# The last mixture of experts: fp32 one-hot rows and undivided fp32 rows in place of three bf16 parts

## The reference, cut to what matters

```python
def moe_apply(x, combine, dispatch, W, b):
    disp = jnp.einsum('sec,sd->ecd', dispatch, x)      # rows of tokens into slots
    h = jnp.einsum('ecd,edf->ecf', disp, W) + b[:, None, :]
    return jnp.einsum('sec,ecf->sf', combine, h)       # weighted, back to tokens

# x: (2, 512, 128) -> 4 groups of 256 tokens; E = 24 experts, C = 22 slots each
def per_group(xf, lw, lb):
    combine, dispatch = top2_dispatch(xf, Wg, C)
    h = moe_apply(xf, combine, dispatch, W1, b1)       # (256, 512)
    h = layer_norm(h, lw, lb)
    h = jax.nn.relu(h)
    return moe_apply(h, combine, dispatch, W2, b2)     # (256, 128)
out = jax.vmap(per_group)(xg, ln_hid_w, ln_hid_b)
return layer_norm(out + x, ln_out_w, ln_out_b)
```

## Time and profile before

| | |
|---|---|
| Runs | 462.73, 463.72, 465.2 us, median 463.72 |
| Profiled execution | 462.69 us, its span 460.9 us |
| TensorE busy, weight loads | 354.5 us (77%), 209.4 us (45%) |
| VectorE, ScalarE, GpSimd busy | 264.5 us, 201.7 us, 114.1 us |
| Mean granted clock of TensorE | 0.885 |
| Moved by DMA | 46.01 MB, mean 100 GB/s |

### The profile page before, as it was taken

How to read it: one execution, slowest core, us unless ns; L and a number is a source line. 1 busy time by engine, 2 the same in 40 slices (tenths; PEclk the granted TensorE clock), 3 DMA queues, 4 the chain that set the end, 5 groups by cost and what they waited for, 6 DMA issues and landing times.

```text
span 460.9 us, 6703 instructions
## 1 busy us (share of the span) xinstructions
PE 354.5 (77%) x2495; PEld 209.4 (45%) x2495; DVE 264.5 (57%) x661; ACT 201.7 (44%) x317; POOL 114.1 (25%) x155
## 2 busy tenths in 40 slices
PE   1797302995189899899999799987873899989970
PEld 0576301995133322233221467554463443677850
DVE  5425500332687598788950758544568947883435
ACT  2332100321040477677778458564624335565210
POOL 2000277156050716311110000010000055462232
PEclk9997555998579999999999779999995799899987
DMA  4599114001326656000000000001999467431232
GB/s 113 152 192 320 46 52 117 13 33 40 105 63 181 143 144 160 1 3 2 2 2 2 0 0 1 1 1 36 371 329 290 148 201 248 152 106 37 60 82 46
DMA packets 35876, 46.01 MB, mean 100 GB/s; under 512 B 4778, under 2 KB 21682, under 8 KB 35844
## 3 DMA queue, kind: packets, MB, share of 16 engines
q1 hardware_dynamic: 33156, 38.57, 29.9%
q0 software_dynamic: 2688, 7.02, 5.3%
HBM read 31.67 MB, written 13.78 MB: 99 GB/s over the span
## 4 chain that ended last, share of the span: by engine, by line
PE 58%; DVE 15%; issue 8%; ACT 6%; DMA 6%; POOL 5%; SPq 1%; POOLq 0%; DVEq 0%; ACTq 0%
PE ps L1397 9%; PE ps L1605 6%; PE ps L1591 5%; PE ps L1566 4%; PE ps L1851 4%; PE ps L1515 3%; PE ps L1574 3%; PE ps L1696 3%; PE ps L1880 3%; DVE early L1210 3%; PE ps L1527 2%; POOL disp_d L538 2%; PE ps L1801 2%; DVE xn L982 2%; PE ps L1786 2%
## 5 line engine op out<-in xcount | busy, mean ns | idle before, releaser
L1210 DVE TENSOR_REDUCE early<-ps 128x1 f32<-128x512 f32 x128 | 81.0, 684 | 15.9 <-PE ps L1566 11.7
L755 ACT ACTIVATE R<-ps 128x1024 f32<-128x1024 f32 x64 | 62.7, 1020 | 24.7 <-PE ps L1591 23.7
L1397 PE MATMUL ps<-ident,R 128*77 128x128 f32 (+1 forms) x224 | 35.3, 296 | 31.8 <-DMA R<-disp_d 24.8
L1397 PEld LDWEIGHTS ps<-ident,R 128*77 128x77 f32 (+1 forms) x224 | 26.7, 152 | 50.4 <-DMA R<-disp_d 25.2
L1566 PE MATMUL ps<-R 72*128 72x512 bf16 x112 | 39.0, 382 | 1.1 <-DVE early L1210 0.2
L1591 PE MATMUL ps<-R 75*128 75x512 bf16 x128 | 37.6, 379 | 1.6 <-DMA R<-R 1.3
L621 POOL DMA_INDIRECT R<-h_d,srow x16 | 16.5, 1033 | 77.3 <-DMA h_d<-ff 70.3
L1605 PE MATMUL ps<-R,vaug 128*9 128x512 f32 x256 | 33.5, 595 | 0.6 <-ACT R L755 0.6
L1179 DVE TENSOR_SCALAR R<-ps,vcol 128x256 f32<-128x256 f32 x16 | 7.0, 479 | 37.7 <-PE ps L1515 37.7
L1566 PEld LDWEIGHTS ps<-R 72*128 72x128 bf16 x112 | 10.8, 96 | 33.1 <-DVE early L1210 23.9
L538 POOL DMA_INDIRECT disp_d<-R,srow x16 | 15.9, 993 | 36.7 <-DVE srow L1125 32.1
(11 more groups left out here) (324 smaller groups left out, 696.2 us busy)
## 6 DMA issues: line engine op xcount, KB each, us to landing
R<-in_L_ffn_W_dram SPq DMA_DIRECT2D x1, 6144.0 KB, 19.9
h_d<-R SPq DMA_DIRECT2D x12, 256.0 KB, 2.8
q_d<-R SPq DMA_DIRECT2D x24, 96.0 KB, 1.9
R<-k_d SPq DMA_DIRECT2D x24, 96.0 KB
R<-q_d SPq DMA_DIRECT2D x8, 288.0 KB
R<-in_L_ffn_w_dram SPq DMA_DIRECT2D x1, 2048.0 KB, 17.1
h_d<-ff SPq DMA_DIRECT2D x6, 256.0 KB, 2.5
disp_d<-R SPq DMA_DIRECT2D x1, 1032.0 KB, 12.8
```

What stands on the lines that cost most here:

```text
L755: s.activation(probs[idx % 4], ps[:, 2 * (idx % 2):2 * (idx % 2) + 2, :].rearrange("p b t -> p (b t)"), ACT.Exp, scale=QK_SCALE).then_inc( ...
L1210: v.tensor_reduce(mcol[:, u, col:col + 1], bank(ring_bank("row", n)), AX.X, ALU.max).then_inc(s1_max, 1)
L1397: return m.transpose(dst, src, ident[0:k, 0:k])
```

## The change

The token rows `xn` and the inner rows `hsum` go into the dispatches as they are, in fp32, and `slot1h` is fp32 as well. The divisions fall away on ScalarE, VectorE and GpSimd, with their semaphores and with the homes of the parts. `slot1h` takes twice the room: seven tiles lie in R0, the eighth in `wx`. The inner rows get eight homes, one for each q; the last two lie where the weights of the first product were, so rows 6 and 7 wait until all first products are done. Each dispatch has one fp32 matmul where there were three bf16 ones. The wait of a hidden group is on `hid_z` (normalised) in place of `hid_p3`.

```diff
-        yparts = R0[:, 4096:5632].bitcast(BF16).rearrange("p (i t d) -> p i t d", i=3, t=T)
-        slot1h = [R0[:, 5632 + CG // 2 * i:5632 + CG // 2 * (i + 1)].bitcast(BF16) for i in range(T)]
+        slot1h = [R0[:, 4096 + CG * i:4096 + CG * (i + 1)] for i in range(T - 1)]
...
-        hsum = [flat(tile)[:, F1 * i:F1 * (i + 1)] for tile in (t2, attn) for i in range(2)]
...
+        slot1h.append(wx[:, :, :].rearrange("p w d -> p (w d)")[:, 0:CG])
+        hsum = [tile[:, F1 * i:F1 * (i + 1)] for tile in (
+            flat(t2), flat(attn), vaug[:, :, :, :].rearrange("p t h d -> p (t h d)"), r1(4096 + 3 * E1 * M1, 2 * F1)) for i in range(2)]
...
@@ GpSimd
-            def last_rest(u):
-                pool.wait_ge(hid_p2, u + 1)
-                g.tensor_tensor(hparts[u % 6][:, 2, :], hsum[u % 4], hparts[u % 6][:, 1, :], ALU.subtract).then_inc(hid_p3, 1)
...
-                if q >= 2:
-                    last_rest(q - 2)
-            last_rest(T - 2)
-            last_rest(T - 1)
...
@@ ScalarE
-                act.wait_ge(ln_out, 5 * T + TB * (b + 1))
-                s.copy(half_of(yparts[:, 0], b), half_of(xn, b)).then_inc(y_parts, 1)
-            for b in range(B):
-                act.wait_ge(y_rest, b + 1)
-                s.copy(half_of(yparts[:, 1], b), half_of(t2, b)).then_inc(y_parts, 1)
...
-            hid_norm(0)
             copy_quad(12)
-            hid_middle(0)
             copy_quad(13)
             hid_std(1)
...
@@ VectorE
-            for i, left in enumerate((xn, t2)):
-                for b in range(B):
-                    dve.wait_ge(y_parts, B * i + b + 1)
-                    rest = yparts[:, 2] if i else t2
-                    v.tensor_tensor(half_of(rest, b), half_of(left, b), half_of(yparts[:, i], b), ALU.subtract).then_inc(y_rest, 1)
...
-                    if q >= 4:
-                        dve.wait_ge(hid_p3, q - 3)
...
+                if q >= 6:
+
+                    dve.wait_ge(h1_mm, BLOCKS * QUADS)
...
@@ TensorE
-                    for part in range(3):
-                        for half in range(2):
-                            ins = m.matmul(ps[:, 6 * (gr % 2) + half, 0:CG // 2], yparts[:, part, gr + TB * b, :],
-                                           slot1h[gr + TB * b][:, half * (CG // 2):(half + 1) * (CG // 2)],
-                                           start=(b == 0 and part == 0), stop=(b == B - 1 and part == 2))
+                    for half in range(2):
+                        ins = m.matmul(ps[:, 6 * (gr % 2) + half, 0:CG // 2], xn[:, gr + TB * b, :],
+                                       slot1h[gr + TB * b][:, half * (CG // 2):(half + 1) * (CG // 2)],
+                                       start=(b == 0), stop=(b == B - 1))
...
-            def dispatch_hidden(gr, f, b, part):
+            def dispatch_hidden(gr, f, b):
                 for half in range(2):
                     ins = m.matmul(ps[:, chunk_bank(4 * gr + f) + half, 0:CG // 2],
-                                   hparts[(2 * gr + b) % 6][:, part, f * P:(f + 1) * P],
+                                   hsum[2 * gr + b][:, f * P:(f + 1) * P],
...
-                pe.wait_ge(hid_p3, 2 * gr + 2)
+                pe.wait_ge(hid_z, 2 * gr + 2)
...
-            pe.wait_ge(hid_p3, T - 1)
-            for part in range(3):
-                for f in range(3):
-                    dispatch_hidden(gr, f, 0, part)
...
+            for b in range(B):
+                pe.wait_ge(hid_z, T - 1 + b)
                 for f in range(3):
-                    dispatch_hidden(gr, f, 1, part)
...
+                    ins = dispatch_hidden(gr, f, b)
+                    if b == B - 1:
+                        ins.then_inc(hdisp_mm, 1)
```

More of the change, by code:

```diff
@@ L1325, in _ @@
                 v.tensor_copy(ring[slot], bank(W1_BANKS[i % 3])).then_inc(h1_dve, 1)
-            def first_rest(u):
-                dve.wait_ge(hid_p1, u + 1)
-                v.tensor_tensor(hsum[u % 4], hsum[u % 4], hparts[u % 6][:, 0, :], ALU.subtract).then_inc(hid_r1, 1)
-            for q in range(T + 1):
-                u = q - 1
+            for q in range(T):
+                t = paired[q]
                 if q == 2:
-                    first_rest(u)
                     add_bias_rows()
-                if q < T:
-                    t = paired[q]
-                    dve.wait_ge(gathered[t], 32)
-                    dve.wait_ge(hb_mm, q + 1)
-                    if q >= 4:
-                        dve.wait_ge(hid_p3, q - 3)
-                    me.link(v.scalar_tensor_tensor(out=hsum[q % 4], in0=got1[q % 4][:, 0, :], scalar=g1[:, 0, t:t + 1],
-                                                   in1=bank(BIAS_BANK[q]), op0=ALU.mult, op1=ALU.add))
-                    second = me.step(v.scalar_tensor_tensor(out=hsum[q % 4], in0=got1[q % 4][:, 1, :], scalar=g1[:, 1, t:t + 1],
-                                                            in1=hsum[q % 4], op0=ALU.mult, op1=ALU.add))
-                if q >= 1 and q != 2:
-                    first_rest(u)
-                if q < T:
-                    me.wait(second)
-                    me.link(v.bn_stats(st6[:, q, :], hsum[q % 4]))
-                    me.link(v.bn_aggr(mv[:, q, :], st6[:, q, :]))
-                    v.tensor_scalar(tmp8b[:, q:q + 1], mv[:, q, 1:2], MOE_EPS, None, ALU.add).then_inc(hvar, 1)
-                if q < T:
-                    dve.wait_ge(hstd, q + 1)
-                    me.link(v.reciprocal(rstd[:, q:q + 1], tmp8[:, q:q + 1]))
-                    v.tensor_scalar(hsum[q % 4], hsum[q % 4], mv[:, q, 0:1], rstd[:, q:q + 1], ALU.subtract,
-                                    ALU.mult).then_inc(hid_z, 1)
@@ new lines, in _ @@
+                dve.wait_ge(gathered[t], 32)
+                dve.wait_ge(hb_mm, q + 1)
+                if q >= 6:
+                    dve.wait_ge(h1_mm, BLOCKS * QUADS)
+                me.link(v.scalar_tensor_tensor(out=hsum[q], in0=got1[q % 4][:, 0, :], scalar=g1[:, 0, t:t + 1],
+                                               in1=bank(BIAS_BANK[q]), op0=ALU.mult, op1=ALU.add))
+                me.link(v.scalar_tensor_tensor(out=hsum[q], in0=got1[q % 4][:, 1, :], scalar=g1[:, 1, t:t + 1],
+                                               in1=hsum[q], op0=ALU.mult, op1=ALU.add))
@@ L1359, in _ @@
+                me.link(v.bn_stats(st6[:, q, :], hsum[q]))
+                me.link(v.bn_aggr(mv[:, q, :], st6[:, q, :]))
+                v.tensor_scalar(tmp8b[:, q:q + 1], mv[:, q, 1:2], MOE_EPS, None, ALU.add).then_inc(hvar, 1)
+                dve.wait_ge(hstd, q + 1)
+                me.link(v.reciprocal(rstd[:, q:q + 1], tmp8[:, q:q + 1]))
+                v.tensor_scalar(hsum[q], hsum[q], mv[:, q, 0:1], rstd[:, q:q + 1], ALU.subtract, ALU.mult).then_inc(hid_z, 1)
             c = 4 * NG - 1
@@ L1919, in _ @@
             for b in range(B):
-                for part in range(3):
-                    ins = dispatch_hidden(gr, 3, b, part)
+                ins = dispatch_hidden(gr, 3, b)
             ins.then_inc(hdisp_mm, 1)
```

42 lines of the change are left out of this document (3 added, 39 removed).

## The result

The changed kernel took 472.06 us in the median of its runs (466.85 to 475.89), the kernel before 464.14 us (462.73 to 465.2) beside it; the ratio is 1.0133 with a 95% interval of 1.0069 to 1.0197. The change makes the kernel slower by some 6 us (0.0133 x 464.14; the medians differ by 7.9). The forecast was 470.6 us, its range 464.8 to 473.0. The profiled execution of the changed kernel took 475.89 us, the longest of its runs and a slow one, while those of the kernel before and of e_after are fast ones. Its first token dispatch starts at 365.31 us where it started at 357.73 before: ahead of it TensorE is busy for 278.0 us with 1459 matmul records, where the same number took 271.2 us before, at a mean granted clock of 0.86 in place of 0.88, in work whose matmuls the change leaves alone.

The account below looks back on a forecast made before the run. The prediction took TensorE to bound the kernel from the first token dispatch on. Its terms, 0.9 + 0.9 + 6.9 - 1.8 = +6.9 us on the median of 463.72, gave 470.6 us, range 464.8 to 473.0.

Parts of the forecast that it names:

- What bounds the region: From first token dispatch to last second product, TensorE is the bound; the removed division is exposed for only 1.8 us.
- A record of fp32: In the dispatches, 264 fp32 columns take 0.223 us per record, two records per matmul: 0.108 us more per replacement.
- the sum of 6.9 for the hidden dispatches: Four hidden groups of 16 fp32 matmuls, 64 at 0.108 us more each, cost 6.9 us.
- The second token pair: Token dispatches of groups 2 and 3, at the full clock: 8 x 0.108 us, a cost of 0.9 us.
- The first token pair: Token dispatches of groups 0 and 1, partly at the low clock until 362.10: cost 0.9 us, up to 1.7.
- Weight loads and one-hot rows at nothing: In the dispatches, fp32 weight loads stay hidden, cost 0; writing one-hot rows in fp32 costs -0.1 to +0.1, taken as 0.
- The waits that go, -1.8: TensorE's waits for GpSimd's division before the first two hidden groups, 0.34 and 1.48 us, vanish: gain 1.8 us, bounds 0 to 1.8.
- One low stretch stays as it is: The low clock from 392.8 to 396.2, inside the first hidden group, keeps its 1.7 us loss; a second would add 1.7.
- the third rival: Around the first hidden group, one more low clock stretch costs 1.7 us, slower records 1.9: 472.3, at most 474; chance 0.10.
- The first rival: TensorE's slow stretch before the last block's copies moves or ends with 160 fewer instructions ahead: 465.1 us; chance 0.16.
- the second rival: In the dispatches, fp32 with one-hot rows takes one pass per record: about 453 to 455 us, faster below 0.158; chance 0.06.
- the fourth rival: TensorE is not the bound and freed engines give more than 1.8 us, at most 2 more: 468.6 us; chance 0.06.

Follow-up runs that it names:

- e_after: The changed kernel run again with no edit, beside the kernel before: 469.91 us, ratio 1.0141.
- e_divide: The changed kernel with the inner rows' division put back on three engines, its parts unused, and hidden groups waiting for it: 472.94 us, ratio 1.0186.
- e_one_part: The kernel before with only the first of three bf16 parts dispatched, the division still running: 463.95 us, ratio 0.9992.
- e_before_wide: The kernel before with the bias matmuls run over 128 partitions, not 24, the added ones times zeros: 459.77 us, ratio 0.9956.
- before with the shorter hold: The kernel before with block 1's gathers held only until quad 3 of the last block is done: 464.19 us, ratio 1.0069.
- e_before_all: The kernel before with 128-partition bias matmuls, 15 dummy matmuls ahead of the first dispatch, and block 1's gathers held until all second products are done: 460.25 us, ratio 0.9963.
- e_before_hold: The kernel before with block 1's gathers held back until TensorE has done all the second products: 462.96 us, ratio 0.9996.
- e_after_dose: The changed kernel with block 0's four gathers moved later, so eight gathers run beside the dense second products: 476.15 us, ratio 1.0256.
- both shorter holds: Each kernel with block 1's gathers held two quads less than until all second products are done: changed kernel 472.41 us, kernel before 464.19 us.
- e_after_wide: The changed kernel with the bias matmuls run over 128 partitions, not 24, the added ones times zeros: 464.9 us, ratio 1.0101.

## Why the prediction was right, step by step

**What bounds the region.** Right for work added: the inner rows' division put back costs some 2 to 3 us (e_divide), while every fp32 group costs its full step. For work taken away it does not hold in the same way: e_one_part gained nothing.

**A record of fp32.** Predicted 0.223 us, measured 0.2225 from start to start at the full clock and 0.440 at the low one. Groups 1, 2 and the last one cost +1.81, +1.82 and +1.91 against 1.73 each: the sum of 6.9 for the hidden dispatches came out as some 7.3. The second token pair cost +0.93 against 0.9.

**The first token pair.** Predicted +0.9 (0.9 to 1.7), measured +0.47 in the ledger. The form did cost what was said: a bf16 pair whose clock rose 3.0 us after its start took 4.29 us (e_before_wide, 356.22 to 359.2), the fp32 pair whose clock rose after 3.3 us took 5.43. But before, the clock rose only after 4.4 us. I held that instant fixed and allowed for a later one only as a loss; an earlier one gives some back. In e_after the same 16 records took 5.97 us.

**Weight loads and one-hot rows at nothing.** Right: 32 records and their loads in 7.39 us, 7.12 of it the records' own pace, leave next to nothing of the loads bare, and the wait for the one-hot rows ahead of the first dispatch is 3.54 us, where it was 3.63.

**The waits that go, -1.8.** Right: no wait before either hidden group, -0.34 and -1.53; the transposes gave 0.27 of it back.

**One low stretch stays as it is.** Wrong, and it is the third rival that happened. In the earlier trace rows it is 3.4 us long; after it is 6.8 us, 399.3 to 406.1, and it is as long in the four further profiles whose work up to there is the changed kernel's (395.5 to 402.3, 393.1 to 399.9, 397.3 to 404.1, 398.6 to 405.4) and in e_divide (394.8 to 401.6). Priced at 1.7 us it shows as +1.0 in the last biases and +0.5 in group 0. That it hangs on the thin matmuls is shown by the four profiles of wide forms, which have none, where all ten with thin ones have it. That it lengthens because of the change is likely but not certain: before with the hold it was 3.4 us, before with the shorter hold 3.4 and later another of 6.8.

**Why the total was still right.** The extra 1.5 us of low clock and 0.4 of the hidden form were set off by what I had not booked: 0.43 less for the first tokens (the earlier clock), 0.50 in block 0's second product, and 1.06 in the tail. The 0.50 is a short pause (from 415.5 on in the kernel before) that e_before_wide and e_before_all have too and e_before_hold has not, though its edit touches nothing there: scatter, and not the change. Most of the 1.06 is another pause, 0.43 us beside block 0's gathers, behind which the small matmuls start again at 430.96, 0.91 us after the last of these gathers had ended. In the changed kernel GpSimd, free of the divisions, ends them at 436.09, 9.5 us before that stage. So this part may be a gain of the freed engines that I had not seen; e_before_wide has no such pause, so it isn't shown. The forecast of +6.9 against +6.84 is thus closer than its terms are; about 2 us of it met by luck. In e_after the same distance is +7.40.

**The tail.** The bursts stayed, as forecast, but the reason was open. GpSimd's gathers beside the 32-column matmuls bring them on. In the earlier trace rows and in the copies above the loss is 4.6 us (9.86 - 5.24) and 4.3 (9.50 - 5.24). The first rival asked whether 160 fewer instructions ahead could move it: e_after_dose shows that the place in the stream does not decide. I also read the earlier trace rows wrongly: 443.54 is not when the last block's first four quads were done. Matmuls and weight loads of the kernel before:

```profile
430.96 8.69 PE L1880 MATMUL ps<-R 128*32 128x128 f32 x294 [0.43 <-issue]
...
439.22 0.17 PEld L1880 LDWEIGHTS ps<-R 128*32 128x32 f32 x6 [0.38 <-issue]
...
443.53 1.28 PEld L1880 LDWEIGHTS ps<-R 128*32 128x32 f32 x33 [1.26 <-issue]
```

The four quads end with the 288th of the 352 matmuls, which started before 438.9. The copy came more than 4 us later, within 0.02 us of the even pace's return: the slow stretch holds ScalarE up as well. The 4.6 us lost stand, since the last copy does follow TensorE's end.

**The fast fp32 form, the second rival.** Refuted by the 0.2225 us. Its threshold had a sign wrong: with 1.8 us of waits won, the two forms are even at (0.3375 + 1.8/80)/2 = 0.180 us a record, not at 0.158, where some 3.6 us would already be won. The measured record is above both.

**The freed engines, the fourth rival.** Their 9.8, 9.0 and 10.1 us (predicted 12, 9 and 9) bought the waits above and at most the pause in the tail.

## What to carry to other kernels

Price an exact fp32 matmul against its bf16 parts by the distance of their records in the same trace, on the engine that bounds, before counting what other engines save: here 2 x 0.2225 us replaced 3 x 0.1125, and 29 us of work taken from three engines did not pay for 80 such exchanges. Work removed from TensorE is only gained as far as its clock stays up and the other engines keep pace; e_one_part took away two thirds of the dispatch records and gained nothing. And look at what GpSimd issues beside short matmuls: moving its gathers away cured the matmuls here, but it pays only if the gathers do not line up behind the end.

## What the runs showed of the hardware

Beside indirect gathers issued by GpSimd, TensorE ran its 128x32 weight loads and 128-column matmuls in bursts of up to six pairs every 0.72 us, where they otherwise follow at 28 ns. In the kernel before the even weight loads stopped at 438.84, 0.9 us after the first gather began (the same lag in the changed kernel, e_after, e_divide, both shorter holds and the first set of e_after_dose), and came back at 443.53, about 1 us after the last had ended. ScalarE was held up with TensorE: in the kernel before, both shorter holds, e_after_dose and e_one_part a copy whose matmuls had long started came only 0.9 to 1.2 us after the last gather's end. The hidden dispatches, one record in 0.2225 us, ran beside block 0's gathers with no loss. So did a single quad of the small matmuls, 32 in 1.02 us from 427.63 on in the kernel before, and in e_after_wide small matmuls for 1.65 us. So in these runs the slow stretch comes only with the gathers, and they are not enough for it.

The bursts are put down to issue, and no semaphore was waited for. The Trainium skill ("Runtime: NRT & Kernel Launch", Instruction fetch mechanics) has the engines' instructions streamed in by DMA and mostly hidden; without gathers the 352 pairs in 9.81 us agree. A late transfer of instructions does not explain the bursts either. The trace lists these transfers as a kind of their own, `instruction`, and all that moved in the kernel before from 438.6 to 445.1, through the whole slow stretch, is this (packets, MB, share of the DMA engines):

```profile
q0 software_dynamic: 128, 0.26, 19.8%
q1 hardware_dynamic: 14, 0.01, 0.3%
```

Which resource the engines share with the gathers stays open.

With the bias matmuls over 24 partitions the clock fell beside or just behind them in all ten profiles, although TensorE hardly paused: 0.34 us before 392.07, and the low stretch from 392.8; at 128 partitions, with the same columns and zeros in the rest, it did not fall there in any of four. The best version measured is the kernel before with that edit: 459.77 us, ratio 0.9956 [0.992, 0.9992].
